# The gated-delta-net step of an AdaLN block, its operations issued in another order within a step on TensorE, ScalarE, VectorE and GpSimd

## The reference

```python
mod = silu(c) @ wmod                       # six vectors for each sequence
h = layernorm(x) * (1 + ca) + sa
x = x + ga * attn(h)
h = layernorm(x) * (1 + cb) + sb
x = x + gb * ffn(h)                        # silu(h@Wg) * (h@Wu), top 2 of 4, @ Wd

# attn: 16 key heads of 128, two value heads of 128 for each
qkv = conv4(h @ W_qkv.T)                   # four causal taps for each channel
q, k = l2norm(q), l2norm(k)
beta, decay = sigmoid(h @ W_b.T), exp(-softplus(h @ W_a.T + dt_bias) * exp(A_log))
for t in tokens:                           # state S: 128 x 128 for each value head
    dv = beta * (v - k @ S)
    S  = S * decay + outer(k, dv)
    o  = q @ S
out = o * rsqrt(mean(o*o) + eps) * norm_w * silu(z)
y = out @ W_out.T
```

## Time and profile before

| what | us |
|---|---|
| median of 3 runs | 1999.02 |
| lowest and highest | 1995.98, 1999.43 |
| profiled execution: span from its first to its last instruction | 1992.6 |
| profiled execution: its own time | not listed apart from the span |
| PE busy in it | 1944.7 |
| DVE busy | 1788.5 |
| ACT busy | 1743.4 |
| POOL busy | 1374.6 |

### The profile page before, as it was taken

One profiled execution on the slowest core, in us unless ns is written; L12 is line 12 of the kernel. 1 busy time (PEld: TensorE's weight loads), 2 busy tenths in 40 slices (PEclk: granted clock), 3 DMA queues, 4 the chain that ended last, 5 costly groups with the idle time before them and its releaser, 6 DMA issues.

```text
span 1992.6 us, 63706 instructions
## 1 busy us (share of the span) xinstructions
PE 1944.7 (98%) x24518; PEld 1655.2 (83%) x24518; DVE 1788.5 (90%) x2907; ACT 1743.4 (87%) x3591; POOL 1374.6 (69%) x957
## 2 busy tenths in 40 slices
PE   7799999999999999999999999999999999998999
PEld 6478888888888888888888888888888888886888
DVE  7789999999999999999999999999999999997987
ACT  7599999999999999999999999999999999997332
POOL 5467777777777777777777777777777777665552
PEclk9799999999999999999999999999999999999999
DMA  3000000000000000000000000000000000002100
GB/s 118 13 24 2 3 24 3 24 2 24 3 24 3 24 3 3 24 3 24 2 24 3 24 3 24 3 3 24 3 24 3 24 3 2 24 7 86 49 17 22
DMA packets 18013, 36.02 MB, mean 18 GB/s; under 512 B 5804, under 2 KB 14508, under 8 KB 15412
## 3 DMA queue, kind: packets, MB, share of 16 engines
q1 hardware_dynamic: 17716, 31.95, 4.7%
HBM read 29.30 MB, written 2.64 MB: 16 GB/s over the span
## 4 chain that ended last, share of the span: by engine, by line
PE 93%; DVE 3%; issue 1%; ACT 1%; POOL 1%; DMA 0%; POOLq 0%; SPq 0%; ACTq 0%; DVEq 0%
PE bank L668 82%; PE bank L671 10%; DVE cc L1877 0%; DVE tt L1752 0%; DVE b_le L1742 0%; DMA o<-in_x 0%; ACT inv L1448 0%; DVE yl L1945 0%; POOL go L556 0%; DVE cols L1836 0%; DVE ae L1916 0%; DVE maskT L1777 0%; POOL a L565 0%; ACT invT L1453 0%; POOL invT L572 0%
## 5 line engine op out<-in xcount | busy, mean ns | idle before, releaser
L1877 DVE SCALAR_TENSOR_TENSOR cc<-bank,wc,cc 128x510 f32<-128x510 f32 (+2 forms) x768 | 558.9, 740 | 11.3 <-ACT cc L1363 1.5
L668 PE MATMUL bank<-h,w 128*128 128x512 f16 (+1 forms) x1920 | 423.3, 361 | 1.2 <-DVE zg L1990 1.1
L668 PEld LDWEIGHTS bank<-h,w 128*128 128x128 f16 x1920 | 174.8, 98 | 137.1 <-issue 6.6
L1448 ACT ACTIVATE inv<-bank 128x512 f16<-128x512 f32 x384 | 244.9, 638 | 16.0 <-PE bank L668 16.0
L500 POOL TENSOR_TENSOR rn<-n2m,mhalf 128x4 f32<-128x4 f32 x64 | 64.5, 1008 | 274.4 <-DVE n2m L1890 274.4
L1453 ACT ACTIVATE invT<-bank 128x512 f16<-128x512 f32 x384 | 246.9, 643 | 2.0 <-PE bank L668 2.0
L1945 DVE TENSOR_TENSOR yl<-bank,mask 128x512 f16<-128x512 f32 x320 | 219.1, 685 | 6.7 <-PE bank L668 6.6
L668 PE MATMUL bank<-inv,a 128*128 128x64 f16 (+1 forms) x3584 | 218.1, 197 | 3.7 <-ACT inv L1448 3.4
L1363 ACT ACTIVATE cc<-bank,wc 128x512 f32<-128x512 f32 x256 | 178.0, 696 | 31.3 <-PE bank L668 31.3
L668 PEld LDWEIGHTS bank<-inv,a 128*128 128x128 f16 x3584 | 180.8, 98 | 16.1 <-ACT inv L1448 4.6
L668 PE MATMUL bank<-w,h 128*128 128x256 f16 x1536 | 190.0, 274 | 0.0
(11 more groups left out here) (235 smaller groups left out, 5486.6 us busy)
## 6 DMA issues: line engine op xcount, KB each, us to landing
w_raw<-in_wh SPq DMA_DIRECT2D x15, 1032.0 KB, 4.9
out<-sol SPq DMA_DIRECT2D x16, 128.0 KB, 1.7
v<-in_x SPq DMA_DIRECT2D x3, 512.0 KB, 3.8
moving<-rank_store SPq DMA_DIRECT2D x64, 8.0 KB
standing<-rank_store SPq DMA_DIRECT2D x64, 8.0 KB
w_raw<-in_wgate SPq DMA_DIRECT2D x1, 1024.0 KB, 4.9
cc<-in_wup SPq DMA_DIRECT2D x1, 1024.0 KB, 5.0
pt<-gate_store SPq DMA_DIRECT2D x2, 512.0 KB, 4.4
```

What stands on the lines that cost most here:

```text
L668: return mm(o_, l_, r_, start=start, stop=stop, skip_group_check=True)
L1448: A(lefts(inv[:, ring(s)], l), halves(bL[0], l), ACT.Copy).then_inc(sig("x_ready"), 1)
L1877: V.scalar_tensor_tensor(dst, src, wc[:, par(s), i, 3 - j:4 - j], dst, ALU.mult, ALU.add).then_inc(sig(f"conv{i}"), 1)
```

## The change

The lists of the four `body` functions are put into another order, and PE's `turn_normed` waits for one more semaphore. No operation is added, taken away or resized; `first_body`, `last_bodies` and all that stands before and behind the steps are the same. The new lists, and the one function that differs (`if s0`, `if s1`... guards left out of the lists, indices in brackets are the level or the part, then the stage):

```diff
 def turn_normed(s):
     need(pe, "kn", N(s) * 4 + 4)
+    if N(s):
+        need(pe, "sq1", N(s) + 1)
```

PE, before and after:

```diff
-project(0) s0, turn_system s1, refine s2, key_cross s1, level_rows(0), project(1) s0,
-first_values s2, level_left(0), turn_values(0) s1, project(2) s0, level_right(0), level_rows(1),
-turn_values(1) s1, project(3) s0, level_left(1), level_right(1), turn_keys s0, key_state s2,
-level_rows(2), first_output s2, turn_output(0) s3, level_left(2), level_right(2),
-turn_queries s0, query_state s2, level_rows(3), second_values s2, decay_product(0) s0,
-turn_output(1) s3, level_left(3), level_right(3), project_output(0) s3, decay_product(1) s0,
-second_output s2, level_rows(4), z_rows(0) s1, turn_normed s0, level_left(4), level_right(4),
-project_output(1) s3, level_rows(5), key_query s0, key_key s0, level_left(5), z_rows(1) s1,
-residue s1, level_right(5)
+turn_system s1, project(0) s0, level_rows(0), refine s2, project(1) s0, level_right(0),
+level_left(0), first_values s2, turn_values(0) s1, level_rows(1), project(2) s0, key_cross s1,
+turn_keys s0, level_left(1), level_right(1), project(3) s0, level_rows(2), turn_values(1) s1,
+first_output s2, key_state s2, level_left(2), level_right(2), turn_output(0) s3,
+query_state s2, level_rows(3), second_values s2, level_left(3), level_right(3),
+turn_queries s0, turn_output(1) s3, level_rows(4), decay_product(0) s0, second_output s2,
+level_right(4), level_left(4), decay_product(1) s0, project_output(0) s3, turn_normed s0,
+project_output(1) s3, level_rows(5), z_rows(0) s1, level_left(5), key_key s0, z_rows(1) s1,
+residue s1, level_right(5), key_query s0
```

ACT:

```diff
-last_tap(0), refined s2, cross_kept s1, split_weights, last_tap(1), first_scaled s2,
-inverse_left(0), scaled_high s2, last_tap(2), queries_high, inverse_right(0),
-values_turned(0) s1, last_tap(3), inverse_left(1), first_kept s2, inverse_right(1),
-values_turned(1) s1, squares(0), first_output s2, output_high(0) s3, inverse_left(2),
-squares(1), query_part s2, inverse_right(2), decay_exp(0), output_high(1) s3,
-inverse_right(3), second_kept s2, inverse_left(3), decay_exp(1), keys_normed,
-output_squares s2, z_tanh(0) s1, keys_turned, inverse_left(4), inverse_right(4),
-level_rows_last, inverse_odds, inverse_left(5), z_tanh(1) s1, high_half, inverse_right(5)
+split_weights, last_tap(0), refined s2, last_tap(1), inverse_left(0), inverse_right(0),
+first_scaled s2, first_kept s2, values_turned(0) s1, last_tap(2), cross_kept s1, squares(0),
+inverse_left(1), scaled_high s2, inverse_right(1), queries_high, last_tap(3),
+values_turned(1) s1, first_output s2, inverse_left(2), inverse_right(2), output_high(0) s3,
+query_part s2, second_kept s2, inverse_left(3), inverse_right(3), output_high(1) s3,
+decay_exp(0), squares(1), keys_normed, decay_exp(1), inverse_left(4), output_squares s2,
+keys_turned, inverse_right(4), level_rows_last, inverse_odds, inverse_left(5),
+z_tanh(0) s1, z_tanh(1) s1, high_half, inverse_right(5)
```

DVE:

```diff
-convolve(0,1), level_rows(0), convolve(0,2), cross_low s1, convolve(0,3), convolve(1,1),
-convolve(1,2), convolve(1,3), level_rows(1), convolve(2,1), convolve(2,2), convolve(2,3),
-convolve(3,1), level_rows(2), second_rest s2, convolve(3,2), squared_norms(0),
-output_low(0) s3, convolve(3,3), level_rows(3), squared_norms(1), guarded_keys,
-guarded_queries, output_low(1) s3, add_output(0) s3, second_output s2, level_rows(4),
-output_sums s2, keys_low, add_output(1) s3, decayed_queries, decayed_keys, z_gate(0) s1,
-correction s1, z_gate(1) s1, first_inverse
+level_rows(0), convolve(0,1), convolve(0,2), convolve(0,3), convolve(1,1), convolve(1,2),
+level_rows(1), convolve(1,3), convolve(2,1), cross_low s1, convolve(2,2), squared_norms(0),
+level_rows(2), convolve(2,3), convolve(3,1), second_rest s2, convolve(3,2), level_rows(3),
+convolve(3,3), output_low(0) s3, guarded_keys, level_rows(4), output_low(1) s3,
+second_output s2, squared_norms(1), add_output(0) s3, output_sums s2, keys_low,
+guarded_queries, add_output(1) s3, decayed_keys, z_gate(0) s1, correction s1, z_gate(1) s1,
+first_inverse, decayed_queries
```

POOL (`gate_output` s3, `unit_system` s1, `first_inverse` s1, `output_scale` s3 stand ahead of both):

```diff
-low_half s1, scaled_low s2, queries_low, scaled_output s3, split_weights, key_norm,
-masked_beta, decay_beta
+scaled_output s3, masked_beta, split_weights, scaled_low s2, queries_low, low_half s1,
+key_norm, decay_beta
```

More of the change, by code:

```diff
@@ L614, in body @@
                     output_scale(s3)
-                if s1 and s0:
-                    low_half(s1)
+                    scaled_output(s3)
+                if s0:
+                    masked_beta(s0)
+                    split_weights(s0)
                 if s2:
@@ L620, in body @@
                     queries_low(s0)
-                if s3:
-                    scaled_output(s3)
+                if s1:
+                    low_half(s1)
                 if s0:
-                    split_weights(s0)
                     key_norm(s0)
-                    masked_beta(s0)
                     decay_beta(s0)
-                if s1 and not s0:
-                    low_half(s1)
+                if s1 and (not s0):
                     for j in range(TL):
@@ L1055, in body @@
                 if s1:
-                    turn_system(s1)
+                    level_rows(0, s1)
                 if s2:
                     refine(s2)
-                if s1:
-                    key_cross(s1)
-                    level_rows(0, s1)
                 if s0:
@@ L1074, in body @@
                 if s1:
[L1075 to L1079, removed]
+                    key_cross(s1)
+                if s0:
+                    need(pe, 'vv', N(s0) * 2 - 1)
+                    turn_keys(s0)
+                if s1:
+                    level_left(1, s1)
+                    level_right(1, s1)
                 if s0:
@@ L1083, in body @@
                 if s1:
[L1084 to L1088, removed]
+                    level_rows(2, s1)
+                    need(pe, 'kx', N(s1) + 1)
+                    need(pe, 'kxl', N(s1) + 1)
+                    turn_values(1, s1)
                 if s2:
+                    first_output(s2)
                     key_state(s2)
                 if s1:
-                    level_rows(2, s1)
-                if s2:
-                    first_output(s2)
+                    level_left(2, s1)
+                    level_right(2, s1)
                 if s3:
@@ L1109, in body @@
                     second_values(s2)
+                if s1:
+                    level_left(3, s1)
+                    level_right(3, s1)
                 if s0:
-                    bank_decays(0, s0, s3)
-                    decay_product(0, s0)
+                    need(pe, 'vv', N(s0) * 2)
+                    turn_queries(s0)
                 if s3:
@@ L1116, in body @@
                 if s1:
-                    level_left(3, s1)
-                    level_right(3, s1)
+                    level_rows(4, s1)
+                if s0:
+                    bank_decays(0, s0, s3)
+                    decay_product(0, s0)
+                if s2:
+                    second_output(s2)
+                if s1:
+                    level_right(4, s1)
+                    level_left(4, s1)
+                if s0:
+                    bank_decays(1, s0, s3)
+                    decay_product(1, s0)
                 if s3:
@@ L1122, in body @@
                 if s0:
[L1123 to L1126, removed]
+                    turn_normed(s0)
+                if s3:
+                    bank_output(1, s0)
+                    project_output(1, s3)
                 if s1:
-                    level_rows(4, s1)
+                    level_rows(5, s1)
                     bank_z(0, s0, s3)
@@ L1133, in body @@
                         turn_hidden(1)
+                    level_left(5, s1)
                 if s0:
[L1135 to L1145, removed]
                     key_key(s0)
                 if s1:
-                    level_left(5, s1)
                     bank_z(1, s0, s3)
@@ L1615, in body @@
                     refined(s2)
+                if s0:
+                    last_tap(1, s0)
+                if s1:
+                    inverse_left(0, s1)
+                    inverse_right(0, s1)
+                if s2:
+                    first_scaled(s2)
+                    first_kept(s2)
+                if s1:
+                    values_turned(0, s1)
+                if s0:
+                    last_tap(2, s0)
                 if s1:
@@ L1618, in body @@
                 if s0:
[L1619 to L1634, removed]
+                    squares(0, s0)
                 if s1:
@@ L1667, in body @@
                     inverse_left(3, s1)
+                    inverse_right(3, s1)
+                if s3:
+                    output_high(1, s3)
                 if s0:
+                    decay_exp(0, s0)
+                    squares(1, s0)
+                    keys_normed(s0)
                     decay_exp(1, s0)
-                    keys_normed(s0)
+                if s1:
```

(13 more changed lines are left out.)

78 lines of the change are left out of this document (37 added, 41 removed).

## The result

| | before | after |
|---|---|---|
| median, us | 1997.5 (4 runs, 1995.0 to 1999.4) | 2086.4 (4 runs, 2083.9 to 2087.5) |
| profiled execution: span | 1992.6 | 2084.3 |
| its own time | not listed | 2086.13 |

The kernel became slower, by a ratio of 1.0441 (95% interval 1.0427 to 1.0456). The forecast was 1991.0 with a range of 1981 to 2011, and faster was given 0.62: wrong in direction and outside the range.

The account below looks back on a forecast made before the run. TensorE was taken to bound the kernel. Steps of 26.97 plus 0.20 us of waits, taken as 27.2, save 8.8 us over 62 steps; with +1 for the first step, 1999.0 - 7.8 = 1991 us, range 1981 to 2011.

Parts of the forecast that it names:

- the 26.68: TensorE's time for a typical step, in us, without its losses: 27.30 less 0.62; claimed to stay unchanged.
- POOL and SP: GpSimd's masked_beta and split_weights move ahead of scaled_low, and the weights' transfer starts earlier; claimed to cost nothing.
- TensorE's blocks: Matmul blocks on TensorE get new predecessors; f32 blocks and transposes bring a step to 26.97 us before waits.
- The old big wait: TensorE's wait at level_left(3) for DVE's level_rows(3): shrinks from 0.22 to 0.08 us, with a DVE chain of 13.45.
- Two new tight places: New TensorE waits: level_rows(4) for inverse_left(3), 0.02 us, and decay_product(1) for output_low(1), 0.10 us.
- rival 3: All TensorE waits go: steps of 26.97 us, kernel at 1978 us; chance 14%.
- ACT: split_weights ahead of last_tap(0) fills ACT's idle time: free in ordinary steps, 0.17 us gained in every fourth.
- First and last step: project(0) now follows turn_system in step 1: +1 us, bounds 0 and +3; last step 0.
- Rival 1: Slower: a PE-DVE loop through the residue and the chain behind first_inverse takes over, +11, 2010 us; chance 24%.

Follow-up runs that it names:

- experiment 2: The kernel before with only guarded_queries moved, from behind guarded_keys to behind keys_low; 2078.17 us, ratio 1.0406.
- experiment 1: The changed kernel with only guarded_queries moved, from behind keys_low to directly behind squared_norms(1); 1976.19 us, ratio 0.9895 to the kernel before.
- experiments 1 to 6: Besides experiment 1 and experiment 2: changed kernel's late call as tensor_reduce, 1976.82 us; old kernel plus unread probe: tensor_scalar 2078.56, tensor_reduce 1996.81, tensor_scalar behind add_output(0) 2007.21.
- experiment 7: The kernel before with only ACT's split_weights moved, from behind cross_kept to ahead of last_tap(0); 2022.92 us, ratio 1.0127.
- experiment 8: The kernel of experiment 1 with ACT's split_weights put back behind refined, in front of last_tap(1); 2023.73 us, ratio 1.0138.

## Why the prediction was wrong

**The step that failed** is the first sentence of the part-by-part account, "No instruction is added or removed, only one wait, so the 26.68 stay". It takes an instruction's length as its own, wherever it stands. ("Cost nothing" under *POOL and SP* is not what failed: experiment 2 has GpSimd's old list and the same loss, experiment 1 its new list and none.) `guarded_queries` was not even given a term: at 0.17 us it seemed too short to matter. Its length depends on what GpSimd does meanwhile, and the change moved it from a moment in which GpSimd is idle into `gate_output`. It grew by 1.86 us and PE lost 1.78. The step intervals account for nearly all of the result: the 63 between the first and the last `turn_system` add up to 1884.99 - 72.03 = 1812.97 us after and 1726.78 before (63 intervals that end at 1797.14), 86.2 of the 91.7 by which the spans differ.

The trace of before held hints, though none in its ordinary steps. In the layer norm ahead of the steps, four `tensor_scalar` calls of 128x256 from SBUF to SBUF take 1.35 us where GpSimd has only operations on four numbers in each partition, and 5.33 where it works on without a gap. Each of these four ends 0.15 us behind the end of a GpSimd operation, one of them behind the second that it met, after 2.13 us:

```profile
13.49 1.35 DVE L1752 TENSOR_SCALAR tt<-osq,b_le 128x256 f32<-128x256 f32 x4
...
19.04 5.33 DVE L1752 TENSOR_SCALAR tt<-zg,b_le 128x256 f32<-128x256 f32 x4
```

In step 0 a `scalar_tensor_tensor` of 128x128 with SBUF operands is listed with 2.44 us; GpSimd's operation beside it ends at 66.53, and it at 66.68:

```profile
64.24 2.44 DVE L1777 SCALAR_TENSOR_TENSOR maskT<-ident,maskT 128x128 f16<-128x128 f16 x1
```

```profile
63.78 2.75 POOL L520 TENSOR_TENSOR e_b<-ae,b_le 128x1024 f32<-128x1024 f32 x1 [2.49 <-ACT ae L1430]
```

It goes the other way too, when VectorE starts first. A GpSimd operation on four numbers in each partition takes 0.25 us at 10.38. At 16.64, 0.15 us behind the start of a VectorE operation with two SBUF inputs, it takes 1.09 and ends at 17.73, that one at 17.68. So being long in this way doesn't belong to VectorE alone:

```profile
16.49 1.19 DVE L1781 TENSOR_TENSOR h<-y_acc,h 128x1024 f16<-128x1024 f32 x1
```

```profile
10.38 0.25 POOL L449 TENSOR_TENSOR b_le<-b_le,eps 128x4 f32<-128x4 f32 x1
...
16.64 1.09 POOL L449 TENSOR_TENSOR b_le<-b_le,eps 128x4 f32<-128x4 f32 x1 [1.59 <-DVE b_le L1745]
```

The Trainium skill states the rule, in SBUF — State Buffer, sections SBUF: two separate sides and Who interferes with whom: VectorE and GpSimd share one pair of SBUF ports, a GpSimd operation holds it for its whole length, and a DVE operation that uses both read ports, or two SBUF inputs against a GpSimd operation that reads SBUF, is blocked until it ends. VectorE: DVE Perf Modes has `tensor_reduce` without a mode that uses both (section The perf-mode tier table) and gives one to an operation with a single source when source and destination are in SBUF and their outermost sizes are both even or equal (section What auto-detection actually checks). By these the outcome of experiments 1 to 6 follows, and their traces agree: 2.03, 2.05 and 0.96 us for `tensor_scalar`, 0.147 for `tensor_reduce`. That it is the ports and their modes, and not another thing that the two engines share, was not measured apart.

**Point by point:**

- *TensorE's blocks*: right. 26.97 us before waits was forecast; experiment 1 has 26.95, and the changed kernel 26.96 without its wait. `first_values` behind `level_left(0)` takes 0.97 (0.98 forecast), `first_output` behind transposes 0.89 (0.89), as PE in experiment 1 shows:

```profile
1052.04 1.13 PE L667 MATMUL bank<-v,tt 128*128 128x128 f32 x8
1053.01 0.60 PE L670 MATMUL bank<-ident,cc 128*128 128x128 f32 x4
...
1058.57 1.06 PE L667 MATMUL bank<-sol,pt 128*128 128x128 f32 x8
1059.46 0.82 PE L667 MATMUL bank<-us,kx 128*128 128x256 f16 x6
...
1061.94 1.14 PE L667 MATMUL bank<-sol,tt 128*128 128x128 f32 x8
1062.92 0.40 PE L667 MATMUL bank<-yl,invT 128*128 128x64 f16 x8
```

- *The old big wait*: right, a little too dear. The forecast chain was 13.45 us; in experiment 1 DVE has 1062.15 - 1048.77 = 13.38. `level_left(3)` comes 0.08 behind the end of `level_rows(3)`, where 0.12 was reckoned, and the f32 block ahead of it takes 1062.92 - 1061.94 = 0.98, which is its length without a wait. DVE:

```profile
1048.77 0.73 DVE L1930 TENSOR_TENSOR inv<-bank,mask 128x512 f16<-128x512 f32 x1
...
1062.15 0.69 DVE L1942 TENSOR_TENSOR yl<-bank,mask 128x512 f16<-128x512 f32 x1
```

- *Two new tight places* (0.02 and 0.10): neither is there. Without the failed term the order has no wait of PE that the view of waits lists, which is rival 3 (1978 us; experiment 1 measured 1976.19). Forecast and rival 3 were mis-weighted too, then, but by 15 us, not by 95.
- *ACT*: right in direction. All steps have one length. That the move of the split is free does not hold in the old order (experiment 7), and in the new one it is worth far more than the 0.17 of fourth steps (experiment 8).
- *First and last step*: first `turn_system` 72.03 for 70.37, 1.66 later, within the bounds of the +1, but it lies between 68.4 and 73.0 in the runs with these lists, so one profile settles little. From the last `turn_system` to the end it is 199.3 us for 195.5, for which 0 was forecast. Kernels with the new lists take 199.3 to 200.6 there, those with the old ones 195.5 to 198.3: some 3 us, whose cause was not looked for.
- Rival 1 had the right kind of place (DVE late, PE waits for it), but put it at the chain behind `first_inverse`. That chain was on time, and its price was 11 us over before where 89 were measured.

## What to carry to other kernels

When a VectorE call is moved, compare what GpSimd does at its old place and its new one. A call that reads and writes SBUF alone with one source, however small, can take as long as the GpSimd operation that it meets, or longer where a second follows without a gap, and neither the view of waits nor the count of instructions shows it: look for one instruction with two very different lengths. Where it can't be moved, another operation that does the same may not be held.

## What was not expected of the hardware

- In the steps the length of a held instruction is set by GpSimd's end within 0.03 us at three places, whether it comes to 2.03, 2.05 or 0.96 us, against 0.17 alone. In the changed kernel this is so in every step behind the first. Long DVE operations with one operand in PSUM are not held: in experiment 1 `y_acc<-y_acc,bank` at 1070.97 and `ae<-e_b,bank` at 1072.10 start while `gate_output` runs (1070.63 to 1073.00) and take 0.68 and 1.22.
- A convolution that waits for the one before takes 0.78 us and a free one 0.65, as the prediction had worked out from the earlier trace rows. In experiment 1 five in a row, three of them held, take 1054.78 - 1051.12 = 3.66; the two rates give 3 x 0.78 + 2 x 0.65 = 3.64. The prediction set this against the Trainium skill, VectorE: DVE Perf Modes, section The DRAIN you can't avoid, by which a semaphore between two operations costs nothing extra, measured there with `tensor_copy`; the runs go with the rows.

```profile
1051.12 3.74 DVE L1874 SCALAR_TENSOR_TENSOR cc<-bank,wc,cc 128x510 f32<-128x510 f32 x5
1054.78 0.68 DVE L1942 TENSOR_TENSOR yl<-bank,mask 128x512 f16<-128x512 f32 x1
```

The fastest version measured is that of experiment 1, 1976.19 us, 1.05% under the kernel before.
